# Forming x + relu(h) - 1 on TensorE in a graph-attention and mixture-of-experts kernel

## The reference, cut to what matters

```python
def gnn(h, adj, W, a):                      # h is the normalized x
    Wh = h @ W
    e = Wh @ a[:D] + swapaxes(Wh @ a[D:], 1, 2)
    e = where(e > 0, e, 0.2 * e)
    alpha = softmax(where(adj > 0, e, -inf))
    return elu(alpha @ Wh)                  # elu(v) = relu(v) + min(exp(v), 1) - 1
x = x + gnn(layernorm(x), adj, W, a)
x = x + ffn(layernorm(x), ...)              # top 2 of 8 experts, 128 -> 512 -> 128 each
```

## Time and profile before

| | |
|---|---|
| timed runs | 441.59, 440.66, 440.71 us; median 440.71 |
| profiled execution | 442.13 us, span 440.3 us, mean granted PE clock 0.991 |
| busy share of the span | PE 93%, PEld 70%, DVE 82%, ACT 73%, POOL 66% |
| chain that ended last | PE 63%, DVE 20%, ACT 5%, DMA 5%, issue 4% |

### The profile page before, as it was taken

How to read it: one execution, slowest core, us unless ns; L and a number is a source line. 1 busy time by engine, 2 the same in 40 slices (tenths; PEclk the granted TensorE clock), 3 DMA queues, 4 the chain that set the end, 5 groups by cost and what they waited for, 6 DMA issues and landing times.

```text
span 440.3 us, 9161 instructions
## 1 busy us (share of the span) xinstructions
PE 407.3 (93%) x2272; PEld 308.3 (70%) x2290; DVE 358.9 (82%) x1410; ACT 321.3 (73%) x760; POOL 289.0 (66%) x292
## 2 busy tenths in 40 slices
PE   7998999889998888999999999999999999999980
PEld 3656666666666665688878888888888888876630
DVE  5689999999998898999887887777778778757683
ACT  2678887888888987688888678778767877866500
POOL 1041777777777777777777777767667657764662
PEclk9999999999999999999999999999999999999996
DMA  5995334333333344443632433322233233297888
GB/s 181 293 390 193 102 115 118 108 103 104 100 101 104 97 128 122 128 133 98 200 99 95 122 102 101 115 90 84 91 90 90 66 84 90 79 289 247 248 310 316
DMA packets 44004, 63.04 MB, mean 143 GB/s; under 512 B 7744, under 2 KB 24512, under 8 KB 43712
## 3 DMA queue, kind: packets, MB, share of 16 engines
q1 hardware_dynamic: 30448, 34.88, 26.5%
q0 software_dynamic: 9344, 20.10, 13.6%
q10 hardware_dynamic: 4176, 7.66, 5.3%
HBM read 27.28 MB, written 26.94 MB: 123 GB/s over the span
## 4 chain that ended last, share of the span: by engine, by line
PE 63%; DVE 20%; ACT 5%; DMA 5%; issue 4%; SPq 1%; POOL 1%; DVEq 0%; ACTq 0%; POOLq 0%
PE bank L1441 7%; PE bank L1455 7%; PE bank L1454 7%; PE bank L1457 7%; PE bank L1445 7%; PE bank L1442 7%; PE bank L1425 3%; PE bank L1433 3%; PE bank L1403 3%; PE bank L1316 3%; DVE xn L1066 3%; PE bank L1401 3%; DVE bn L901 2%; DVE neg_max L1048 2%; DVE score L1043 2%
## 5 line engine op out<-in xcount | busy, mean ns | idle before, releaser
L520 POOL DMA_INDIRECT expert_slots<-rows,slot_i x128 | 126.4, 987 | 55.4 <-issue 33.5
L712 ACT ACTIVATE yb<-bank,b_sb 128x512 f32<-128x512 f32 x36 | 24.8, 688 | 51.8 <-PE bank L1457 51.8
L1454 PE MATMUL bank<-hh,w_hi 128*128 128x512 f32 x144 | 60.1, 417 | 0.0
L1441 PE MATMUL bank<-xh,w_hi 128*128 128x512 f32 x144 | 58.5, 406 | 0.9 <-ACT xh L697 0.5
L1455 PE MATMUL bank<-hh,w_lo 128*128 128x512 f32 x144 | 57.4, 398 | 0.0
L1445 PE MATMUL bank<-xl,w_hi 128*128 128x512 f32 x144 | 56.9, 395 | 0.2 <-DVE xl L1122 0.2
L1457 PE MATMUL bank<-hl,w_hi 128*128 128x512 f32 x144 | 56.8, 395 | 0.3 <-DVE hl L1153 0.3
L1442 PE MATMUL bank<-xh,w_lo 128*128 128x512 f32 x144 | 56.8, 395 | 0.0
L536 POOL DMA_INDIRECT moe_rows<-hrelu,ysi x40 | 41.2, 1030 | 17.6 <-issue 10.7
L536 POOL DMA_INDIRECT moe_rows<-hexp,ysi x40 | 40.9, 1023 | 17.7 <-issue 10.1
L1146 DVE CAST hh<-z 128x512 fp32r<-128x512 f32 x36 | 16.5, 459 | 42.3 <-ACT z L702 41.9
(11 more groups left out here) (166 smaller groups left out, 1051.0 us busy)
## 6 DMA issues: line engine op xcount, KB each, us to landing
rows<-xn SPq DMA_DIRECT2D x32, 256.0 KB
xs<-expert_slots SPq DMA_DIRECT2D x27, 260.0 KB
x_all<-x SPq DMA_DIRECT2D x16, 256.0 KB, 3.5
w_raw<-w_t SPq DMA_DIRECT2D x2, 2048.0 KB, 13.7
w_raw<-moe_rows SPq DMA_DIRECT2D x16, 256.0 KB, 4.5
out<-x_all ACTq DMA_DIRECT2D x16, 256.0 KB, 4.7
xs<-expert_slots ACTq DMA_DIRECT2D x11, 260.0 KB
w_hi<-moe_rows SPq DMA_DIRECT2D x9, 256.0 KB, 4.1
```

Source lines behind the costliest of these rows:

```text
L520: nc.gpsimd.indirect_dma_start(out=slots, out_offset=bass.IndirectOffsetOnAxis(ap=slot_i[q][:, k * SUB + j:k * SUB + j + 1], axis=0), in_= ...
L712: nc.scalar.activation(yb[:, :], ps_y[:, :], ACT.Identity, bias=b2_sb[:, e:e + 1]).then_inc(yb_ok, 1)
L1441: nc.tensor.matmul(ps_h[c][:, :], w1_hi[:, e, chunk], xh[:, :], start=True, stop=False)
L1454: nc.tensor.matmul(ps_y[:, :], w2_hi[:, e, c, :], hh[:, c, :], start=c == 0, stop=False)
```

## The change

Four things change in the attention stage, all but the memset in its steps.

1. On PE a new function `elu_plus(g1)` stands behind z. It waits for hrelu and hexp of the group and writes x + hrelu - 1 into ps_av, the bank that the attention product was in, by three accumulated matmuls (identity times x, identity times hrelu, and a bf16 identity times a constant -1).
2. `elu_sum` and `residual` are replaced in the steps by `residual_plus`: x = min(hexp, 1) + ps_av in one operation, which waits for the matmuls. The last group keeps the two old operations in the drain.
3. The eight fillers ahead of `norm_turns` go, and wh (g0) moves behind `norm_turns`.
4. On ACT the first of the four exponentials of a group is issued one step earlier, ahead of `turned_norm`; the copy of wh moves from there to behind the other three, ahead of `turned_prob`. The first norm's root of step t + 1 (step 0 only) stands ahead of that first exponential.

The waits for a buffer's free state follow: hrelu and the next attention product wait for x2_ok (the residual) of the group before.

```diff
-FILL_STEP, FILL_NORM = 3, 8
+FILL_STEP = 3
...
@@ ACT
-            def softmax_exp(g1):
+            def softmax_exp(g1, subs):
...
+            def copy_wh(g1):
+
+                act.wait_ge(wh_ps, g1 + 1)
+                if later(g1):
+                    act.wait_ge(av_ps, g1)
+                nc.scalar.copy(wh[:, :, :], tiles(ps_wh)).then_inc(wh_ok, 1)
...
-                    act.wait_ge(u_ok, g1)
+                    act.wait_ge(x2_ok, g1)
...
-                    softmax_exp(g1)
+                    softmax_exp(g1, range(1, SUB))
...
                 if g1 is not None:
+                    copy_wh(g1)
                     turned_prob(g1)
...
+                if isinstance(t, int) and t + 1 < len(BATCHES):
+                    first_root(t + 1)
                 if g0 is not None:
-                    act.wait_ge(wh_ps, g0 + 1)
-                    nc.scalar.copy(wh[:, :, :], tiles(ps_wh)).then_inc(wh_ok, 1)
+                    softmax_exp(g0, range(1))
                 if gx is not None:
                     turned_norm(gx)
-                if isinstance(t, int) and t + 1 < len(BATCHES):
-                    first_root(t + 1)
@@ DVE
+            nc.vector.memset(minus_b[:, :], -1.0).then_inc(ones_ok, 1)
...
+            def residual_plus(gx):
+
+                dve.wait_ge(hexp_ok, gx + 1)
+                dve.wait_ge(plus_ps, gx + 1)
+                nc.vector.scalar_tensor_tensor(x_all[:, bass.ds(gx, 1), :, :].rearrange("p g s d -> p (g s) d"),
+                                               hexp[:, :, :], 1.0, tiles(ps_av), ALU.min, ALU.add).then_inc(x2_ok, 1)
...
-                if gx is not None:
-                    elu_sum(gx)
...
-                    residual(gx)
+                    residual_plus(gx)
@@ PE
                 if later(g1):
-                    pe.wait_ge(hexp_ok, g1)
+                    pe.wait_ge(x2_ok, g1)
...
+            def elu_plus(g1):
+
+                pe.wait_ge(hrelu_ok, g1 + 1)
+                pe.wait_ge(hexp_ok, g1 + 1)
+                if not later(g1):
+                    pe.wait_ge(ones_ok, 2)
+                nc.tensor.matmul(ps_av[:, :], ident, x_all[:, g1, :, :].rearrange("p s d -> p (s d)"), start=True, stop=False)
+                nc.tensor.matmul(ps_av[:, :], ident, hrelu[:, :, :].rearrange("p s d -> p (s d)"), start=False, stop=False)
+                nc.tensor.matmul(ps_av[:, :], ident_b[:, :], minus_b[:, None, :].to_broadcast([P, SUB, P]), start=False, stop=True
+                                 ).then_inc(plus_ps, 1)
...
+                if g1 is not None:
+                    elu_plus(g1)
+                if gx is not None:
+                    if later(gx):
+                        pe.wait_ge(xn2_t_ok, gx)
+                    norm_turns(gx, q)
                 if g0 is not None:
                     ...
                     last.then_inc(wh_ps, 1)
                 if gx is not None:
-                    if later(gx):
-                        pe.wait_ge(xn2_t_ok, gx)
-                    fill(ps_t3, FILL_NORM)
-                    norm_turns(gx, q)
                     gates(gx, ps_gate)
```

More of the change, by code:

```diff
@@ L101, in gnn_moe_kernel @@
         ones_b = sb("ones_b", [P, P], BF16)
+        minus_b = sb("minus_b", [P, P], BF16)
         log_v = sb("log_v", [P, BATCH, SUB])
@@ L273, in gnn_moe_kernel @@
         hexp_ok = sem("hexp_ok")
+        plus_ps = sem("plus_ps")
         u_ok = sem("u_ok")
@@ L605, in softmax_exp @@
                     act.wait_ge(prob_ps, g1)
-                for j in range(SUB):
+                for j in subs:
                     nc.scalar.activation(prob[:, j, :], score[:, j, :], ACT.Exp, bias=neg_max[:, j:j + 1],
                                          accum_out=psum_row[:, j:j + 1]).then_inc(exp_ok, 1)
+            def copy_wh(g1):
[3 more added lines that the diff above has]
+                nc.scalar.copy(wh[:, :, :], tiles(ps_wh)).then_inc(wh_ok, 1)
             def turned_prob(g1):
@@ L717, in drain @@
                 last = GROUPS - 1
-                softmax_exp(last)
+                softmax_exp(last, range(1, SUB))
+                copy_wh(last)
                 turned_prob(last)
@@ L888, in residual @@
             def residual(gx):
-                dve.wait_ge(u_ok, gx + 1)
+                dve.wait_ge(u_ok, 1)
                 nc.vector.scalar_tensor_tensor(x_all[:, bass.ds(gx, 1), :, :].rearrange("p g s d -> p (g s) d"),
```

## The result

The changed kernel takes 445.08 us (median of 5 runs, 444.51 to 446.18) where the kernel before takes 440.71 (5 runs, 440.61 to 441.59) beside it on the same chip: a ratio of 1.0098, 95% interval 1.0077 to 1.0119. The forecast was 442.1, range 440.9 to 443.6: the sign was right, the size was not. The profiled execution took 446.18 us with a span of 444.4.

A forecast was written before the change was run, and what follows sets the result against it. No engine is full in the attention stage; a ring of waits, 10.16 us per step, bounds it. First steps +1.8, steady +0.6, steps 14 and 15 -0.5, hand-over -0.5: +1.4 on 440.71 gives 442.1 us, range 440.9 to 443.6.

The forecast's parts named there:

- The steady steps: Steps 4 to 13: the residual, waiting for elu_plus, comes 0.06 us later per step; +0.6 in all, bounds 0 and +1.6.
- elu_plus is late in each step: Rival: the wait on exp keeps weights from loading ahead, +0.16 a step, or a two-semaphore wait costs more; 443.3 us, chance 0.18.
- theory A: Formed after the measurement: in steady steps elu_plus's wait for exp is still open, so weights load late; 0.17 of the 0.27.
- Step 4: Counted among the ten steady steps, 4 to 13, at +0.06 us each.
- The first steps: Steps 1 to 3: elu_plus, added whole, delays wh and step 2's early fillers; z of group 3 +1.8 us, bounds +1.4 to +2.0.
- Steps 14 and 15: ScalarE's ring: second norm's transpositions start sooner, but elu_plus holds the residual; -0.5 us for both steps, bounds 0 and -0.9.
- Hand-over: From the last z to the experts: gates start 3.18 us after it instead of 3.70; -0.5 us, bounds -0.3 and -0.6.
- a shift of the stage's end passes through whole: From about 185 us on, unchanged instructions form one chain, so any shift of the attention stage's end reaches the kernel's end.
- At nothing: Terms costed at zero: residual reading PSUM, memset of -1, first exponential moved ahead, wh's copy moved, hrelu's wait for x2.
- VectorE as the bound: Rival: removing VectorE's separate elu sum shortens each step by up to 0.74 us; about 432.9 us, chance 0.06.
- The clock: Rival: without the eight fillers TensorE's clock falls to its lower level, +8 us for each of ten steps; 520 us, chance 0.02.

The follow-up runs named there:

- e3: Changed kernel, but VectorE forms elu's sum and the residual as before; the three passes still run and nobody waits for them: 441.46 us, ratio 1.0013.
- e1: Changed kernel with wh of g0 put back ahead of elu_plus on TensorE: 456.07 us in one execution.
- e8: Changed kernel with the three passes in the same place but into the turned probabilities' bank, waiting for the relu alone: 443.18 us, ratio 1.0055.
- e9: e7 without the three fillers of each step from step 3 on: 439.46 us, ratio 0.9957 to the kernel before.
- e2: Changed kernel without step 2's nine early fillers and the three between its transpositions: 444.21 us, ratio 1.0075.
- e5: Changed kernel with x's pass made right after attention, all passes in the turned probabilities' bank, those behind z waiting for relu alone: 445.86 us, ratio 1.01.
- e7: e5 without step 2's fillers, with z ahead of TensorE's ranks, its copy ahead of ScalarE's exponential, VectorE's load statistics ahead of counts: 442.59 us, ratio 1.0028.
- e4: e3 without elu_plus, so the kernel before with the changed order alone and the eight fillers gone: 442.69 us, ratio 1.0042.

## Why the prediction was wrong, by its steps

*The steady steps: the step that failed.* The prediction gave +0.06 a step, with +0.16 as a bound "if TensorE's weights can't be loaded ahead", and took the 0.06 because it let elu_plus start at 101.07 with no delay. Measured: +0.27. The mechanism was the one named as a bound and as the rival "elu_plus is late in each step" (443.3, chance 0.18), and e3 shows that it is the residual's wait for the passes that costs; what failed is the size of the term. It has three parts. The load of weights behind the open wait costs 0.17 (a gap of 0.09 and 0.08 on the first pass; both are gone in e1 and e8), not 0 and not the 0.10 that the attention product showed. The road over z's end costs the 0.06 that was forecast. The remaining 0.04 is VectorE's row behind the residual, whose operation chosen takes 0.27 us (101.95) instead of 0.23 in the kernel before; its cause is open.

The rows of the kernel before could have warned of it. Exp ends at 101.02 and z's last product has issued at 101.07 there. In the changed kernel this is no accident of one step: hrelu starts at 102.47, 0.08 behind the inverse sum (102.22 + 0.17 = 102.39; the attention product that its row names had ended at 101.65). VectorE writes the inverse sum just ahead of chosen_b, and on chosen_b z's chain starts (102.53). In the kernel before the inverse sum and the attention product, for which hrelu waits as well, end within 0.04 us of each other:

```profile
97.64 1.16 PE L1337 MATMUL bank<-wh,prob_t 128*128 128x128 f32 x8 [0.24 <-ACT prob_t L615]
98.59 0.17 DVE L1080 RECIPROCAL inv_sum<-psum_row 128x4 f32<-128x4 f32 x1
```

So the two roads to the passes start together, and the wait for exp is still open when TensorE comes to it. Of theory A's rivals, longer float passes are excluded by the spacing of 0.86 in e1 and e8, the order by e3, and the scatters by e9, whose steps of 9.59 are shorter than the scatters' 10.12.

Over steps 5 to 13 the miss is 9 x 0.21 = 1.9 of the 2.7 us by which the sum was missed (4.1 against 1.4).

*Step 4* was counted as a steady one. It is 10.74: VectorE stands 0.52 us between the residual (44.17) and its statistics (45.37) where it is 0.16 elsewhere. The same 0.52 stands at the same place, the residual of group 2, in every kernel with the new residual (e1, e2 and e5 to e9, though in e7 and e9 step 4 is no longer than its neighbours), and not in the kernel before, e3 and e4, which have the old one. So it goes with the new residual's code, and not with the passes. Its 0.3 us stay unexplained; nothing was tried on it.

*The first steps: right.* +1.8 forecast, +2.0 measured. The instants fit: elu_plus at 21.23 (forecast 21.50, and this run's first z is 0.33 early), the last transposition of prob at 27.04 (27.25), hrelu at 29.18 (29.46), the residual at 33.79 (33.90). Two causes were put together there, and e2 parts them: 1.26 go with the fillers, 0.74 stay. z of group 3 (42.00) lies where it was forecast, 1.8 behind its old place (40.3), or 0.2 later than that if the early start is taken off.

*Steps 14 and 15: half right.* -0.5 forecast, -0.25 measured. e3 shows the gain of the order whole, -0.64, and e8, where the weights are loaded in time, -0.58. The difference to the measured -0.25, 0.33 in two steps, is the size of the same late load, 0.17 a step, which the forecast left out of this term as well.

*Hand-over: right in the gates.* They start 169.84 - 166.60 = 3.24 us after the last z (forecast 3.18, before 3.70). That all of what lies behind that z became 0.4 shorter (forecast 0.5) agrees but shows little: it compares one execution of each kernel, and executions of the changed kernel alone lie 1.7 us apart. The prediction's sentence that a shift of the stage's end passes through whole held here, but not in e9, where 3.6 of 6.1 us were lost.

*At nothing:* reading a bank costs the residual nothing that these rows can resolve: it takes 0.69 us from a bank (107.07) and 0.68 from SBUF. The estimate of 0.065 us more in each step, worked out in the prediction from the Trainium skill ("VectorE: DVE Perf Modes", the section on the TRN2 errata), is not in this trace. That VectorE had 0.78 us of idle time ahead of the score, and no u, was as forecast: the time that the change gives VectorE is worth nothing, as z does not come sooner.

*The rivals.* VectorE as the bound: shown wrong by that idle row. The clock: it holds in the changed kernel, but e4 shows that without fillers and passes it can fall. The forecast set 520 us for the whole stage at the lower level; in e4 it was one step, 12.22 instead of 10.16, so +2 us. The prediction cited the Trainium skill ("TensorE: Matmul & The Clock Gate", "Why this matters for your kernels") against long idle gaps; here the clock fell behind a stretch in which TensorE idled for 1.2 us at the longest, so the row and not the rule decides.

## What to carry to other kernels

Work moved onto an engine costs first by where it stands in that engine's queue: three passes of one form cost a steady step nothing when nobody waits for them (e3), 0.27 us when the residual does, and 0.72 more when wh's products are put ahead of them (e1). Where two releases tie (here exp's end and z's), don't count the later one at zero: here the product whose wait was still open had its weights loaded only afterwards, and the cheap cure was to take the reason for the wait away (another bank, e8). That gave 0.16 us back between z and the residual, of which 0.09 were left in the step. And before filling an engine's idle time, look for it in the first and last steps too: idle time that is there in the middle of a loop was not there at its ends.

## What was not expected of the hardware

The 1.9 us of three passes in a step can be what holds TensorE's clock: with nothing in their place (e4 against e3) it fell to the lower level for at least 5 us behind a stretch in which TensorE was busy 5.9 of 8 us, while an earlier stretch with 5.7 of 8 passed without a fall. The first of two float passes, when its wait ends just as TensorE comes to it, costs 0.17 us more than behind a wait that is already met (e1, e8): 0.09 in its start and 0.08 in its length. GpSimd's scatters take 0.96 us with 0.30 between them, and one in each group of eight takes 1.29 in the changed kernel (105.76); why was not found.
